# Split products for every expert weight, one two further back: a one-core patch, attention and routed-expert kernel

## Chip, core and metric

The kernel runs on one core of a Trainium2 chip. The metric is the device time in microseconds (us) of one execution; the profile covers one execution, and its span is a little shorter than the time that is reported for it.

## What is computed

The reference, cut to its steps (64 images, 114 tokens each: a class token, 36 patches, 77 text tokens; width 256):

```
h = concat(patches @ W + b with class token + positions, txt)     # 64 x 114 x 256
h = h + linear_attention(layernorm(h))                            # 16 heads, elu + 1
x = layernorm(h); logits = x @ gate_w.T                           # 8 experts
sel = argmax(logits); rw = sigmoid(max(logits))
for e in range(8):                                                # one expert per token
    xs = x * (rw * (sel == e))
    out += (xs @ w_up[e].T) * silu(xs @ w_gate[e].T) @ w_down[e].T
return h + out                                                    # inner width 128
```

## The kernel before

**Stages.** 18 units make the patches. Then a loop of 32 steps (`step(i)` on each engine, all written out) runs the attention of 32 pairs of images as a pipeline: in step i TensorE projects pair i, applies attention to pair i-1, projects pair i-2 out and ranks the experts' choices of pair i-4. The 64 rows of attention output per pair go to a scratch tensor in HBM, sorted by expert, with two indirect DMAs per pair, which GpSimd issues (`scatter`, L674). The last stage walks over 64 tiles of 128 sorted rows, two tiles at a time: a "two" is called `duo` in the code, there are 32 of them (`DUOS`), and `duo_step(j)` is one engine's part of a round. All tiles of one expert lie together, so each tile has one expert, read from a table into registers.

**A two in the last stage.** SyncE loads its two tiles from the scratch. TensorE transposes the rows (`turn_rows`, L1687), ScalarE copies them out rounded (`xsT_hi`, L967), VectorE makes the rest (`xsT_lo`, L995). TensorE multiplies by gate and up (`gate_up`, L1400 to L1402), ScalarE takes the silu of the gate half (L961), VectorE scales the up half and multiplies (`act_of`, L1296). TensorE transposes that (`turn_act`, L1674), ScalarE copies it (`actT`, L956), TensorE multiplies by the down weight (`down`, L1701), VectorE adds the rows (`result_of`, L1308), and GpSimd stores the result with one indirect DMA per tile (L760).

**Split parts.** `product` (L1400 to L1402) writes one float32 product as three products of rounded operands: high by high, high by low, low by high. Before the change it is used everywhere but in `down`, which multiplies in float32; the trace shows two matmul records for each of its products. The high parts of the gate and up weights are made by ScalarE (L874) and the low parts by GpSimd (L683), one of 16 pieces in each of the steps 10 to 25.

**Order.** Nothing schedules: the order on each engine is that of the code, and semaphores hold the engines together. In the last stage TensorE runs in each round gate and up of tile 0, the transposes of the two before, gate and up of tile 1, `down` of the two before, and the transposes of the rows two ahead. The last pairs of the attention and the first twos are interleaved by hand.

**Tables.** When 23 pairs are ranked, a table of the first 32 tiles is made ("early"): VectorE counts in step 27 (`early_count`), and works out row and expert of each tile in steps 28 and 29 (`early_slots`, `early_rows`). SyncE can then load tiles. The other 32 tiles need all pairs: `late_count` on TensorE waits until GpSimd has added up the last choices (`so_far`, L658, in `count_chosen`), then VectorE works out the late table in `late_count`, `late_slots` and `late_rows`. GpSimd's own order at the end of the attention is `scatter` of pair 30, `count_chosen` of pair 31, `scatter` of pair 31, and only then the stores.

## Time and profile before

| | |
|---|---|
| time, median of 3 runs | 437.87 us (436.64 to 438.05) |
| the profiled execution | 436.53 us, span 434.7 us |
| TensorE busy | 412.7 us, 95% of the span |
| VectorE busy | 349.8 us, 80% |
| ScalarE busy | 283.1 us, 65% |
| GpSimd busy | 298.6 us, 69% |
| 64 stores on GpSimd (L760) | 62.3 us busy, 28.4 us idle before them |

How to read it: an engine's busy share is a mean over stages. A row of the timeline gives the start and the length of an operation, and in brackets how long its engine stood idle before it and what ended that. Matmuls overlap, so what a matmul costs TensorE is the distance between starts and not its length.

### The profile page before, as it was taken

What the parts mean: (1) busy time and instruction counts of PE and PEld (TensorE: products, weight loads), DVE (VectorE), ACT (ScalarE), POOL (GpSimd) and SP (SyncE); (2) the same over time, 40 slices, a digit from 0 to 9 for tenths busy, and PEclk for the clock granted to TensorE, in tenths of its full rate; (3) what the DMA queues carried; (4) which work ended last, traced back from release to release, by engine and by line L of the source; (5) the groups of instructions that cost most, each with busy time, mean ns of one, the idle gap of its engine ahead of it and who ended that gap; (6) DMA issues with size and microseconds to landing.
All of it is one profiled execution on the core that took longest, in us unless ns stands there. A gap on an engine that the chain in (4) does not pass through costs nothing.

```text
span 434.7 us, 13221 instructions
## 1 busy us (share of the span) xinstructions
PE 412.7 (95%) x4325; PEld 398.7 (92%) x4325; DVE 349.8 (80%) x1147; ACT 283.1 (65%) x688; POOL 298.6 (69%) x678
## 2 busy tenths in 40 slices
PE   7999999999999999999999999999997999999980
PEld 6999899999999999999999999989896998999970
DVE  5678568999999999999999999998886766766650
ACT  5554476788688788788778778766664554555530
POOL 4065214677878888888888888776677777666662
PEclk9999999999999999999999999999999999999995
DMA  7974122333422321231311211128612797222120
GB/s 268 348 250 146 52 48 57 95 93 94 115 71 67 90 68 40 66 96 39 111 53 36 59 55 40 51 74 226 185 45 69 235 288 238 98 73 72 70 78 14
DMA packets 34148, 46.46 MB, mean 107 GB/s; under 512 B 8842, under 2 KB 25856, under 8 KB 34082
## 3 DMA queue, kind: packets, MB, share of 16 engines
q1 hardware_dynamic: 24860, 30.50, 23.2%
q0 software_dynamic: 9216, 15.12, 11.1%
q8 instruction: 36, 0.59, 0.6%
q14 instruction: 30, 0.25, 0.2%
q10 hardware_dynamic: 6, 0.00, 0.0%
HBM read 26.87 MB, written 17.17 MB: 101 GB/s over the span
## 4 chain that ended last, share of the span: by engine, by line
PE 85%; DVE 5%; issue 4%; ACT 1%; DMA 1%; POOL 1%; POOLq 0%; SPq 0%; DVEq 0%
PE b_kg L1400 8%; PE b_kg L1401 8%; PE b_kg L1402 8%; PE b_w L1400 7%; PE b_w L1401 7%; PE b_w L1402 6%; PE b_att L1515 6%; PE b_t L1465 3%; PE b_w L1701 3%; PE b_v L1402 3%; PE b_v L1400 3%; PE b_v L1401 3%; PE b_att L1701 3%; PE b_att L1452 3%; PE b_t L1529 3%
## 5 line engine op out<-in xcount | busy, mean ns | idle before, releaser
L674 POOL DMA_INDIRECT sorted_rows<-rows,place x64 | 75.5, 1180 | 20.3 <-issue 9.4
L760 POOL DMA_INDIRECT out<-result,rows_all x64 | 62.3, 973 | 28.4 <-DVE result L1308 14.7
L866 ACT ACTIVATE q_exp<-b_w,bq_s 128x228 f32<-128x228 f32 x64 | 28.9, 452 | 28.6 <-PE b_w L1402 28.6
L1400 PE MATMUL b_kg<-wgu_hi,xsT_hi 128*128 x128 | 41.3, 323 | 0.5 <-issue 0.4
L1296 DVE SCALAR_TENSOR_TENSOR act_u<-b_kg,rows_all,silu_g 128x128 f32<-128x128 f32 x64 | 19.4, 345 | 27.1 <-ACT silu_g L961 26.7
L1400 PE MATMUL b_w<-xnT_hi,wq_hi 128*128 128x264 f32 x128 | 39.5, 309 | 1.3 <-DVE logits L1119 1.0
L1400 PE MATMUL b_kg<-wkgv_hi,xnT_hi 128*114 128x264 f32 x128 | 38.7, 302 | 0.4 <-DVE patch_out L1036 0.4
L1401 PE MATMUL b_kg<-wkgv_lo,xnT_hi 128*114 128x264 f32 x128 | 36.5, 285 | 0.0
L1401 PE MATMUL b_w<-xnT_lo,wq_hi 128*128 128x264 f32 x128 | 36.4, 285 | 0.0
L1402 PE MATMUL b_kg<-wkgv_hi,xnT_lo 128*114 128x264 f32 x128 | 36.4, 284 | 0.0
L1402 PE MATMUL b_w<-xnT_hi,wq_lo 128*128 128x264 f32 x128 | 36.4, 284 | 0.0
L1402 PE MATMUL b_v<-wkgv_hi,xnT_lo 128*114 128x256 f32 x128 | 36.0, 282 | 0.0
L1400 PE MATMUL b_v<-wkgv_hi,xnT_hi 128*114 128x256 f32 x128 | 36.0, 281 | 0.0
L1402 PE MATMUL b_kg<-wgu_hi,xsT_lo 128*128 x128 | 35.9, 281 | 0.0
L1401 PE MATMUL b_kg<-wgu_lo,xsT_hi 128*128 x128 | 35.8, 279 | 0.0
L1401 PE MATMUL b_v<-wkgv_lo,xnT_hi 128*114 128x256 f32 x128 | 35.7, 279 | 0.0
L1515 PE MATMUL b_att<-kv_sb,qT 128*114 128x136 f32 x256 | 34.9, 279 | 0.7 <-DVE qT L1097 0.7
L1401 PE MATMUL b_w<-wo_lo,attnT_hi 128*114 128x264 f32 x124 | 35.2, 284 | 0.0
L1400 PE MATMUL b_w<-wo_hi,attnT_hi 128*114 128x264 f32 x124 | 35.2, 284 | 0.0
L1402 PE MATMUL b_w<-wo_hi,attnT_lo 128*114 128x264 f32 x124 | 35.0, 283 | 0.0
L821 ACT ACTIVATE xn<-rows_all,shift,rstd 114x255 f32<-114x255 f32 x64 | 34.7, 596 | 0.0
L1515 PEld LDWEIGHTS b_att<-kv_sb,qT 128*114 128x114 f32 x256 | 31.7, 178 | 1.0 <-DVE kv_sb L1088 1.0
(233 smaller groups left out, 1561.7 us busy)
## 6 DMA issues: line engine op xcount, KB each, us to landing
rows_all<-sorted_rows SPq DMA_DIRECT2D x64, 130.0 KB, 3.2
rows_all<-in_x SPq DMA_DIRECT2D x18, 384.0 KB, 4.7
rows_all<-in_txt SPq DMA_DIRECT2D x32, 154.0 KB
rows_all<-in_wgu_in SPq DMA_DIRECT2D x8, 256.0 KB, 3.0
rows_all<-patch_out SPq DMA_DIRECT2D x48, 36.0 KB
sorted_rows<-tail_rows SPq DMA_DIRECT2D x9, 130.0 KB, 2.9
sorted_rows<-rows,place POOLq DMA_INDIRECT x64, 3.7
wdown<-in_wdown_in SPq DMA_DIRECT2D x2, 512.0 KB, 4.5
```

Source lines behind the costliest of these rows:

```text
L674: G.indirect_dma_start(out=scratch[0:EXPERTS * REGION, :], out_offset=bass.IndirectOffsetOnAxis(ap=place[:, k, b:b + 1], axis=0), in_=rows ...
L760: G.indirect_dma_start(out=out, out_offset=bass.IndirectOffsetOnAxis(ap=rows_all[:, t.n, ID:ID + 1].bitcast(I32), axis=0), in_=result[:, k ...
L821: last = S.activation(xn[:, b, 1:], rows_all[0:TOK, 2 * p + b, 1:D], ACT.Identity, bias=shift1[:, p % 8, b:b + 1], scale=rstd1[:, p % 8, b ...
L866: S.activation(q_exp[:, c, :], at, ACT.Exp, bias=bq_s[:, c:c + 1])
L1296: last = V.scalar_tensor_tensor(act_u[:, t.slot(4)], b_gu[m.slot(2)][:, up:up + INNER], rows_all[:, t.n, GAIN:GAIN + 1], silu_g[:, t.slot( ...
L1400: T.matmul(to, left_hi, right_hi, start=start, stop=False, skip_group_check=seeded)
L1401: T.matmul(to, left_hi, right_lo, start=False, stop=False, skip_group_check=seeded)
L1402: return T.matmul(to, left_lo, right_hi, start=False, stop=stop, skip_group_check=seeded)
L1452: last = T.matmul(b_kv[j * PART:(j + 1) * PART, b * KC + c], k_sb[:, b, at:at + PART], v_sb[:, b, c, j, :], start=True, stop=True)
L1465: last = T.transpose(turn_attn_bank(p)[:, at:at + TOK], attn[:, b, c * P:(c + 1) * P], ident[0:TOK, 0:TOK])
L1515: last = T.matmul(b_att[0:TOK, b, c * KVW:(c + 1) * KVW], qT[:, c, b * TOK:(b + 1) * TOK], kv_sb[:, b * KC + c].rearrange("p j w -> p (j w ...
L1701: last = T.matmul(down_bank(m)[:, t.slot(2) * D:(t.slot(2) + 1) * D], actT[:, t.slot(6)], wdown[:, bass.ds(e, 1), :], start=True, stop=True)
```

## The change

Four things are changed. (1) `down` is also written with `product`: the down weight and the activations get high and low parts. ScalarE copies the high part of one expert's down weight and GpSimd subtracts the low part in each of the steps 21 to 28, and the split of gate and up moves from steps 10 to 25 to steps 5 to 20. The activations' high part is ScalarE's copy after the transpose, and VectorE gets a new operation for the low part (`act_low`). (2) In the last stage `down` and `result_of` run two twos behind gate and up instead of one. Each tile of a two has a bank of its own for gate and up, and GpSimd waits for each tile's result by itself. (3) ScalarE scales both halves (a second activation, Identity), so that VectorE's `act_of` is one multiplication of two operands in SBUF, 128 by 256. (4) The sums of the early table move from VectorE to GpSimd, as additions in halves; `late_count` stands one round later.

```diff
-        wdown = sb("wdown", [P, EXPERTS, D])
-        xsT_lo = sb("xsT_lo", [P, 6, KC, P], F32R)
-        actT = sb("actT", [P, 6, P])
+        wdown_hi, wdown_lo = parts("wdown", [P, EXPERTS, D])
+        up_g = sb("up_g", [P, 4, INNER])
...
+        def gate_up_bank(m, n):
+            return b_kg[:, n, m.slot(2) * 2 * INNER:(m.slot(2) + 1) * 2 * INNER]
...
-        GU_STEPS, DOWN_STEPS = (8, 9, 11, 12, 14, 15, 17, 18), (22, 24)
-        GU_SPLIT_STEPS = range(10, 10 + EXPERTS * KC)
+        GU_STEPS, DOWN_STEPS = (8, 9, 11, 12, 14, 15, 17, 18), (20, 21)
+        GU_SPLIT_STEPS, DOWN_SPLIT_STEPS = range(5, 5 + EXPERTS * KC), range(21, 21 + EXPERTS)
...
 GpSimd
+            def down_low(e):
+                pool.wait_ge(down_hi_done, e + 1)
+                G.tensor_tensor(wdown_lo[:, e, :], down_raw(e), wdown_hi[:, e, :].bitcast(F32), ALU.subtract).then_inc(down_lo_done, 1)
...
+            def early_past():
+                pool.wait_ge(early_past_ready, 1)
+                early_link(G.tensor_tensor(past_n[:], past[:], over_slots(ends[:, 0, EXPERTS:2 * EXPERTS]), ALU.mult), 1)
+            def early_sums():
+                for n, width in enumerate((EXPERTS // 2, EXPERTS // 4, EXPERTS // 8)):
+                    G.tensor_tensor(past[:, :, 0:width], past[:, :, 0:width], past[:, :, width:2 * width], ALU.add)
+                    early_link(G.tensor_tensor(past_n[:, :, 0:width], past_n[:, :, 0:width], past_n[:, :, width:2 * width], ALU.add), 2 + n)
+            def early_rows():
+                early_link(G.tensor_scalar(slot_r[:], past_n[:, :, 0], -float(P), None, ALU.mult), 5)
+                early_link(G.tensor_tensor(slot_r2[:], slot_r[:], slots_s[:, EARLY_TILES * EXPERTS:], ALU.add), 6)
+                early_link(G.tensor_scalar(slot_s[:], past[:, :, 0], float(REGION), None, ALU.mult), 7)
+                early_link(G.tensor_tensor(slot_r[:], slot_s[:], slot_r2[:], ALU.add), 8)
+                G.tensor_copy(slot_row[:, 0:EARLY_TILES], slot_r[:])
+                G.tensor_copy(slot_expert[:, 0:EARLY_TILES], past[:, :, 0]).then_inc(early_ready, 1)
...
+                if i == EARLY_PAIRS + 5:
+                    early_past()
+                if i == EARLY_PAIRS + 6:
+                    early_sums()
+                    early_rows()
...
-                    pool.wait_ge(result_ready, m.upto())
                     for t in tiles_of(m):
                         k = t.slot(RESULT_RING)
+                        pool.wait_ge(result_ready, t.n + 1)
...
 ScalarE
+            def act_high(m):
+                act.wait_ge(turn_a_done, m.upto())
+                if m.had(3):
+                    act.wait_ge(down_done, m.upto(3))
+                S.copy(act_parts(m)[0], turn_a_bank(m)).then_inc(actT_hi_ready, 1)
+            def gate_and_up(m):
+                for t in tiles_of(m):
+                    act.wait_ge(gu_done, t.n + 1)
+                    bank, gain = gate_up_bank(m, t.slot(2)), rows_all[:, t.n, GAIN:GAIN + 1]
+                    S.activation(silu_g[:, t.slot(4)], bank[:, 0:INNER], ACT.Silu, scale=gain)
+                    S.activation(up_g[:, t.slot(4)], bank[:, INNER:], ACT.Identity, scale=gain).then_inc(silu_ready, 1)
             def duo_step(j):
+                if j.within(DUOS):
+                    gate_and_up(j)
                 if (j - 1).within(DUOS):
+                    act_high(j - 1)
                 if (j + 2).within(DUOS):
+                    rows_high(j + 2)
...
 VectorE
-                dve.wait_ge(silu_ready, m.upto())
+                dve.wait_ge(silu_ready, m.upto(per=DUO))
...
-                for t in tiles_of(m):
-                    up = t.slot(2) * D + INNER
-                    last = V.scalar_tensor_tensor(act_u[:, t.slot(4)], b_gu[m.slot(2)][:, up:up + INNER], rows_all[:, t.n, GAIN:GAIN + 1],
-                                                  silu_g[:, t.slot(4)], ALU.mult, ALU.mult)
-                last.then_inc(act_ready, 1)
+                V.tensor_tensor(duo(act_u, m), duo(up_g, m), duo(silu_g, m), ALU.mult).then_inc(act_ready, 1)
+            def act_low(m):
+                dve.wait_ge(actT_hi_ready, m.upto())
+                high, to = act_parts(m)
+                low(to, turn_a_bank(m), high).then_inc(actT_lo_ready, 1)
...
                 if j.within(DUOS):
                     act_of(j)
                 if (j - 1).within(DUOS):
-                    result_of(j - 1)
+                    act_low(j - 1)
+                if (j - 2).had(2) and (j - 2).within(DUOS):
+                    result_of(j - 2)
                 if (j + 2).within(DUOS):
                     rows_low(j + 2)
...
 TensorE
             def gate_up(m, n):
+                if m.had(1):
+                    pe.wait_ge(silu_ready, DUO * (m.n - 1) + n + 1)
...
             def down(m):
-                pe.wait_ge(actT_ready, m.upto())
+                pe.wait_ge(actT_lo_ready, m.upto())
...
-                    last = T.matmul(down_bank(m)[:, t.slot(2) * D:(t.slot(2) + 1) * D], actT[:, t.slot(6)],
-                                    wdown[:, bass.ds(e, 1), :], start=True, stop=True)
+                    last = product(down_bank(m)[:, t.slot(2) * D:(t.slot(2) + 1) * D], [part[:, at] for part in act_parts(m)],
+                                   (wdown_hi[:, bass.ds(e, 1), :], wdown_lo[:, bass.ds(e, 1), :]), True, True)
...
                     first_products(m)
-                    gate_up(m, 0)
+                    for n in range(DUO):
+                        gate_up(m, n).then_inc(gu_done, 1)
                 if (j - 1).within(DUOS):
                     turn_act(j - 1)
-                if m.within(DUOS):
-                    gate_up(m, 1).then_inc(gu_done, 1)
-                if (j - 1).within(DUOS):
-                    down(j - 1)
                 if (j + 2).within(DUOS):
                     turn_rows(j + 2)
+                if (j - 2).had(2) and (j - 2).within(DUOS):
+                    down(j - 2)
...
             down(Turn(0, 1))
             rank(PAIRS - 1)
-            late_count()
             turn_rows(Turn(0, 4))
             duo_step(Turn(0, 3))
+            late_count()
+            duo_step(Turn(0, 4))
             late_slots()
```

How the order moves on TensorE within one round of the last stage. Before, the piece from the end of gate and up to the next transposes of rows (`wdown` is the down weight, `actT` the activations, `con_s` holds the identity with which TensorE transposes, ISA rows compute an address):

```order
L1402 MATMUL b_kg<-wgu_hi,xsT_lo 128x256
L1654 ISA
L1701 MATMUL b_w<-wdown,actT 128x256
L1654 ISA
L1701 MATMUL b_w<-wdown,actT 128x256
L1687 MATMUL b_t<-con_s,rows_all 128x128 x4
L1654 ISA
L1400 MATMUL b_kg<-wgu_hi,xsT_hi 128x256
```

The same place of the changed kernel, from the last product of gate and up to the first of the second tile's down (`wkgv_lo` and `xnT_hi`, `xnT_lo` are the attention's tiles, used again for the rows' low part and for the activations' two parts):

```order
L1493 MATMUL b_kg<-wgu_hi,wkgv_lo 128x256
L1768 MATMUL b_w<-con_s,act_u 128x128 x2
L1781 MATMUL b_t<-con_s,rows_all 128x128 x4
L1745 ISA
L1491 MATMUL b_att<-wdown_hi,xnT_hi 128x256
L1492 REGISTER_ALU
L1492 MATMUL b_att<-wdown_lo,xnT_hi 128x256
L1493 MATMUL b_att<-wdown_hi,xnT_lo 128x256
L1745 ISA
L1491 MATMUL b_att<-wdown_hi,xnT_hi 128x256
L1492 REGISTER_ALU
```

The 12 products of gate and up now stand in one run, both kinds of transposes stand together, and the down products, six where there were two, stand last, of the two before the one whose activations are being transposed.

On TensorE where the attention ends. Before, behind the ranking of the last pair (`chosen`, `so_far`):

```order
L1433 MATMUL b_att<-chosen,earlier 114x16
L1434 MATMUL b_att<-chosen,ones_bf 114x8
L1436 MATMUL b_att<-so_far,ones_bf 114x16 x2
L1734 MATMUL b_att<-so_far,ones_bf 1x8 x2
L1736 MATMUL b_att<-ones_bf,so_far 8x1 x2
L1687 MATMUL b_v<-con_s,rows_all 128x128 x4
```

In the changed kernel, the end of round 3, which stands between that ranking and `late_count`:

```order
L1493 MATMUL b_kg<-wgu_hi,wkgv_hi 128x256
L1768 MATMUL b_w<-con_s,act_u 128x128 x2
L1781 MATMUL b_t<-con_s,rows_all 128x128 x4
L1828 MATMUL b_att<-so_far,ones_bf 1x8 x2
L1830 MATMUL b_att<-ones_bf,so_far 8x1 x2
L1742 TENSOR_LOAD slot_expert
```

The two sums that need the last `so_far` have moved behind the transposes of rows of two 4, the products of two 3, the activations' transposes of two 2 and the rows' transposes of two 5.

On VectorE at the same time. Before, behind the statistics of the last pair (`BN_AGGR`):

```order
L1049 BN_STATS stats<-rows 114x6 x2
L1053 BN_AGGR mv<-stats 114x2 x2
L1296 SCALAR_TENSOR_TENSOR act_u<-b_kg,rows_all,silu_g 128x128 x2
L1308 SCALAR_TENSOR_TENSOR result<-rows_all,b_w 128x256 x2
L995 TENSOR_TENSOR xsT_lo<-b_v,xsT_hi 128x512
```

The same place after the change:

```order
L1141 BN_STATS stats<-rows 114x6 x2
L1145 BN_AGGR mv<-stats 114x2 x2
L1087 TENSOR_TENSOR xnT_lo<-b_w,xnT_hi 128x256
L1375 TENSOR_TENSOR act_u<-up_g,silu_g 128x256
L1391 SCALAR_TENSOR_TENSOR result<-rows_all,b_w 128x256 x2
L1087 TENSOR_TENSOR wkgv_hi<-b_v,xsT_hi 128x512
```

The low part of two 1's activations (`xnT_lo<-b_w`), for which `down` of two 1 waits, stands behind the statistics of the last pair; before, that product waited for ScalarE's copy alone.

## Rows read from the trace of the kernel before

**Rows 1.** Timeline, TensorE, one two: start us, length us, engine, line, operation.

```profile
369.30 0.36 PE L1400 MATMUL b_kg<-wgu_hi,xsT_hi 128*128 x1
369.50 0.28 PE L1401 MATMUL b_kg<-wgu_lo,xsT_hi 128*128 x1
...
370.09 0.38 PE L1674 MATMUL b_w<-con_s,act_u 128*128 128x128 f32 x2
...
371.03 1.12 PE L1701 MATMUL b_w<-wdown,actT 128*128 x4
371.99 0.60 PE L1687 MATMUL b_t<-con_s,rows_all 128*128 128x128 f32 x4
372.35 0.36 PE L1400 MATMUL b_kg<-wgu_hi,xsT_hi 128*128 x1
```

**Rows 2.** Timeline, VectorE, the same two; idle time and its releaser in brackets.

```profile
368.83 0.61 DVE L1296 SCALAR_TENSOR_TENSOR act_u<-b_kg,rows_all,silu_g 128x128 f32<-128x128 f32 x2 [0.98 <-ACT silu_g L961]
369.35 0.86 DVE L1308 SCALAR_TENSOR_TENSOR result<-rows_all,b_att 128x256 f32<-128x256 f32 x2
370.20 0.69 DVE L995 TENSOR_TENSOR xsT_lo<-b_v,xsT_hi 128x512 fp32r<-128x512 f32 x1
```

**Rows 3.** Timeline, ScalarE, the same two.

```profile
370.51 0.37 ACT L956 COPY actT<-b_w 128x256 f32<-128x256 f32 x1 [0.34 <-PE b_w L1674]
371.21 0.63 ACT L961 ACTIVATE silu_g<-b_kg,rows_all 128x128 f32<-128x128 f32 x2 [0.34 <-PE b_kg L1402]
372.63 0.59 ACT L967 CAST xsT_hi<-b_t 128x512 fp32r<-128x512 f32 x1 [0.78 <-PE b_t L1687]
```

**Rows 4.** Timeline, GpSimd: first store, 24th store, last store of 64.

```profile
336.96 1.01 POOL L760 DMA_INDIRECT out<-result,rows_all  x1 [0.30 <-issue]
...
366.40 0.97 POOL L760 DMA_INDIRECT out<-result,rows_all  x1 [0.30 <-issue]
...
426.38 0.97 POOL L760 DMA_INDIRECT out<-result,rows_all  x1 [0.30 <-issue]
```

**Rows 5.** Timeline, TensorE and VectorE, around the wait for so_far.

```profile
327.78 0.25 DVE L1053 BATCH_NORM_AGGREGATE mv<-stats 114x2 f32<-114x6 f32 x2
...
330.62 0.19 PE L1734 MATMUL b_att<-so_far,ones_bf 128*1 128x8 bf16 x2 [2.45 <-POOL so_far L658]
```

**Rows 6.** Chain of waits: the eight products of apply in steps 25, 26 and 30.

```profile
257.20 0.93 PE b_att L1515 x8
...
265.45 0.93 PE b_att L1515 x8
...
300.72 0.93 PE b_att L1515 x8
```

**Rows 7.** Busy time by stretch, VectorE: the early table's parts in steps 28 and 29.

```profile
278.85:280.30 1.45, 1.35 (x9) 1.00 0.00 0
287.95:289.06 1.11, 1.01 (x9) 1.00 0.00 0
```

**Rows 8.** Timeline, GpSimd: a weight's low part, start of step 30, its top_n.

```profile
260.80 0.74 POOL L683 TENSOR_TENSOR wgu_lo<-rows_all,wgu_hi 128x256 fp32r<-128x256 f32 x1
...
296.12 0.23 POOL L635 TENSOR_SCALAR ve<-mv 114x2 f32<-114x2 f32 x1 [0.56 <-DVE mv L1053]
...
301.94 0.20 POOL L650 TENSOR_TENSOR top_n<-top,ratio 114x2 f32<-114x2 f32 x1
```

**Rows 9.** Timeline, ScalarE: a tanh of step 31, the only table load of the late stage.

```profile
305.85 0.24 ACT L805 ACTIVATE tanh_top<-top_n 114x2 f32<-114x2 f32 x1
...
315.50 1.28 ACT L974 ACT_TABLE_LOAD   x1
```

**Rows 10.** Timeline, GpSimd and VectorE: a scatter and a read beside qT.

```profile
280.78 1.25 POOL L674 DMA_INDIRECT sorted_rows<-rows,place  x1 [0.33 <-POOL place L671]
...
280.85 0.62 DVE L1097 SCALAR_TENSOR_TENSOR qT<-q_exp,q_relu 128x456 f32<-128x456 f32 x1
...
306.04 0.64 DVE L1097 SCALAR_TENSOR_TENSOR qT<-q_exp,q_relu 128x456 f32<-128x456 f32 x1
...
306.16 0.58 POOL L642 TENSOR_TENSOR ratio<-spread,rstd 114x2 f32<-114x2 f32 x1
```

More of the change, by code:

```diff
@@ L1382, in _ @@
             stats_2(PAIRS - 1)
-            duo_step(Turn(0, 2))
+            act_low(Turn(0, 1))
+            act_of(Turn(0, 2))
+            result_of(Turn(0, 1))
+            rows_low(Turn(0, 4))
             places(PAIRS - 1)
+            duo_step(Turn(0, 3))
             late_count()
-            duo_step(Turn(0, 3))
+            duo_step(Turn(0, 4))
             late_slots()
-            duo_step(Turn(0, 4))
+            duo_step(Turn(0, 5))
             late_rows()
-            straight(range(5, DUOS + 1), duo_step)
+            straight(range(6, DUOS + 2), duo_step)
         @block.tensor
```

137 lines of the change are left out of this document (79 added, 58 removed).

## The prediction

> **What bounds the kernel now.** I read the timeline of TensorE first, because it is busy for 95% of the span. In the last stage one round (two tiles) lasts from 369.30 to 372.35, which is 3.05 us, without a gap [rows 1]. Inside it, six products of gate and up take 0.79 us (369.30 to 370.09). The next piece, transposes of the activations and six more products, takes 0.94, so the transposes cost 0.15. `down` takes 0.96 (371.03 to 371.99) and the rows' transposes 0.36. The spacing of the products is (370.09 - 369.50) / 5 = 0.118 us, and the first after transposes takes 0.20. VectorE works 0.61 + 0.86 + 0.69 = 2.16 us in such a round and idles 0.98 before one of them [rows 2]. ScalarE works 0.37 + 0.63 + 0.59 = 1.59 us [rows 3].
>
> The second thing to see is GpSimd's stores. The first starts at 336.96, the 24th at 366.40: 29.44 / 23 = 1.280 us each, back to back, although TensorE had produced results before [rows 4]. So GpSimd starts late, behind the last scatters, and catches up, since two stores take 2.56 us and a round 3.05. From then on it follows TensorE. The 64th store starts at 426.38, that is 89.4 us after the first, where 63 x 1.280 = 80.6 would do. The end of the kernel is 434.7 - 426.38 = 8.3 us after that start. Two limits therefore lie close together: 3.05 us per round on TensorE, 2.56 on GpSimd.
>
> The third view is the chain of waits in the loop. From step 25 to 26 the distance of `apply` is 265.45 - 257.20 = 8.25 us; from there to step 30 it is 35.27 instead of 4 x 8.25 = 33.0 [rows 6]. In those steps VectorE makes the early table, in stretches of 1.45 and 1.11 us [rows 7]. VectorE is nearly full in this loop, so the work goes straight into the step. Last, TensorE stands 2.45 us until 330.62 for the last `so_far` [rows 5].
>
> **The change, part by part.**
>
> *Down in split parts, order within a round.* After the change a round on TensorE is 12 products in one run that follows products (12 x 0.118 = 1.42), activations' transposes 0.15, rows' transposes 0.36, and six products behind transposes 0.79: 2.72 us, so 0.33 less than now [rows 1]. Over the 26 rounds from 5 to 31 that is 8.6 us on TensorE alone.
>
> *Will the others keep up with 2.72?* ScalarE gets two more activations. The pair costs 0.63 [rows 3]; two pairs 1.26, with 0.37 and 0.59 that makes 2.22. If the second of each kind did not overlap, four would cost about 1.46 and the sum is 2.42. Silu and Identity alternate per tile; a table load costs 1.28 us, but the only one of this stage is at 315.50 and Identity, Tanh and Silu all follow it without another [rows 9], so I count none. VectorE: `act_of` becomes one operation of 256 columns and `act_low` is one from PSUM of 256. Neither stands in the trace; 512 columns take 0.69 and 128 about 0.31 [rows 2], so each lies between 0.31 and 0.69, and I take 0.41. Sum 0.41 + 0.41 + 0.86 + 0.69 = 2.37 of 2.72. With bounds it is 2.17 to 2.93; only the upper end would be a new limit. The distances between engines get longer by one stage, but `down` now asks for activations of two rounds ago: a chain of silu, `act_of`, transposes, copy and low part (about 0.34 + 1.3 + 0.4 + 0.15 + 0.34 + 0.37 + 0.4 = 3.3 us) has over 5 us. So I keep 2.72 on TensorE.
>
> *The stores.* Now GpSimd needs 2.56 for a round of 2.72, and it starts about three rounds behind. It gains only 0.16 us per round on TensorE, so over 29 rounds it just about catches up. The end is then set by the first store plus 80.6 us, with almost no idle left. I put TensorE's round 5 at about 334.8 and round 31 at 334.8 + 26 x 2.72 + 0.6 (two loads of the tables) = 406.1; the results of two 29 come some 4.1 us later, at 410.2. GpSimd, if it starts at 335.9 (below), wants them at 335.9 + 29 x 2.56 = 410.1. So 0.2 us idle. This replaces 89.4 by 80.8: **-8.6 us**. It also caps the gain: a still faster TensorE would bring nothing.
>
> *Late count moved.* The wait of 2.45 us for `so_far` goes, since two 3 is multiplied in between. What is late next is `act_low` of two 1: it stands on VectorE behind the statistics of the last pair, which end at 327.78 + 0.25 [rows 5]. With 0.41 more, `down` of two 1 starts at 328.45, takes 0.79, and with the ranking TensorE is at the rows of two 4 at 329.4 where it now is at 330.8: -1.4 us. Two 2 is no longer in front of round 4, which shifts work to the end, where TensorE is not the limit. None of this moves the first store, which waits for GpSimd's own scatters; it keeps the results ahead of the stores.
>
> *Early table on GpSimd.* From VectorE go 1.45 + 1.11 us; `early_share` (about 0.6: a small operation and one of 256 elements) comes back. So 2.0 of the 2.27 us lost in steps 26 to 30 can return. But GpSimd pays. A low part costs 0.74 [rows 8], and three more steps get one; the multiplication in step 28 has as many elements per partition, 0.74 too. The halving sums have 128, 64 and 32 elements, twice each; between 0.20 (an operation of two elements) and 0.74 (256) these are about 0.46, 0.33 and 0.26, so 2.1 for the six, four linked small ones at 0.31 and two copies 0.4: with links 3.8 to 4.3 us in step 29. After it GpSimd has only 0.56 us of idle before step 30 [rows 8], so step 30 starts about 3.6 us later than now, and its top_n (301.94) ends at about 305.7. The tanh that needs it runs at 305.85 now [rows 9], and keys and values of step 31 stand behind it on ScalarE. At that point the 1.9 us that VectorE won are held up to the old time; part of it comes back in the idle time that ScalarE has behind it. For the first store I take -1.1 us, with bounds of -2.0 (all is kept) and +1 (GpSimd is later still).
>
> *Costs at nothing.* The down weights' 8 copies on ScalarE and the earlier split of gate and up: hidden by ScalarE's waits for TensorE in each step; if that cover were gone, about 0.4 us per step. The down weights' loads: they leave SyncE's queue behind the text of steps 19 and 20 and are wanted in steps 21 and 25. The later early table lets the first tiles load later; they are wanted after step 31.
>
> **Sum.** First store 336.96 - 1.1 = 335.9; last store + 80.8 = 416.7; + 8.3 = 425.0 us span, which is 9.7 less than 434.7. The profiled execution took 436.53, so 426.8 for its like. The median of the runs lies 1.3 above the profiled one, the lowest run 0.1; I add 0.9 and predict **427.7 us**.
>
> **A lock that speaks against it.** `act_of` now reads both operands from SBUF. What such an operation does to GpSimd shows beside `qT`, which has two SBUF operands as well: GpSimd's `ratio` took 0.58 us beside it (306.16, [rows 10]), where an operation of its form takes 0.20 [rows 8]. A scatter that ran over the whole of another `qT` took 1.25 [rows 10]; I see no stretching of DMA issues. If each store pair were held for the 0.41 us of `act_of`, a round would cost GpSimd 2.97, and the last store would start at 335.9 + 31 x 2.97 + 1.28 = 429.3: 2.9 us later than now.
>
> The Trainium skill, page "SBUF — State Buffer", section "Who interferes with whom", says that a VectorE instruction with two SBUF inputs contends with a GpSimd instruction that reads SBUF, not with one that only writes it, and that whichever came second waits. The stretched `ratio` agrees with it. By its sentence that descriptor generation needs the write side, which it calls inferred, the stores are not held; if their reads of indices counted, the second number holds.
>
> **Rivals.**
> - *As above:* 425.9 to 429.0 us, chance 0.60.
> - *The loop gives nothing or takes.* GpSimd's debt in step 29 holds ScalarE, and the first store stays at 337 or comes at 338: 428.8 to 430. For it: 3.6 us of debt against 0.56 of idle. Against it: the idle times of step 31. Chance 0.17.
> - *The round is longer than 2.72:* at 2.80 to 2.90 the results of two 29 come 2 to 5 us later and GpSimd waits for them: 429.8 to 433. For it: VectorE at its upper bound (2.93). Chance 0.12.
> - *ScalarE becomes the bound and the kernel is slower.* If it does not run ahead and each of its three groups waits the hop from TensorE again (0.34, 0.34, 0.78), the round is 2.42 + 1.46 = 3.9 us. It decides against the change from a round of about 3.35 us on. At 3.5, 27 x 0.45 - 1.4 = 10.8 us are added to TensorE's time: 448. Against it: those waits are there only because ScalarE is ahead. Chance 0.04.
> - *The lock holds the stores:* 437.87 + 2.9 = 440.8 by the number above, chance 0.03.
> - *Nothing comes of it:* six products cost as much as the four records did, and the loop breaks even: 437 to 438.5. Against it: 0.118 per product is measured for the same operands. Chance 0.04.
>
> The measurement of this kernel can tell about 0.3% (1.3 us) from no change. Faster by more: 0.60 + 0.17 + 0.12 and a little of the last, 0.90. Within: 0.03. Slower: 0.07. The range is 425.0 (loop gain kept whole, no starving) to 431.0 (the first of the two slower cases of the gain, half of the next): that leaves out the far half of the third case and those below it.
>
> **What would show it.** In the changed profile: six down products spaced 0.118 apart; rounds of 2.72 on TensorE, with no idle; 64 stores over 80.6 to 81.5 us, each pitch 1.28 with next to no waits for VectorE; the first store at about 335.9; no wait for `so_far` but a wait of some 1.3 us in front of `down` of two 1; `apply` of steps 26 to 30 less than 34 us apart, and ScalarE waiting for top_n in step 31. I am wrong if a pitch above 1.4 stands beside `act_of`, if table loads appear, or if TensorE waits in most rounds for VectorE or ScalarE.

## The result, and the profile after

The changed kernel takes **431.27 us** in the median of 4 executions (430.77 to 431.85), the kernel before 437.44 us beside it; the ratio is 0.986, 95% interval 0.9834 to 0.9885. It is faster, by about 6.2 us. Forecast were 427.7 us, range 425.0 to 431.0. The profiled execution took 431.59 us, its span is 429.8. One execution of the kernel before, of 580.02 us at a granted clock of 0.654, was in a slower state and is left out of every median and ratio.

The page of the changed kernel, its stores group (operation, busy time, mean ns of one, idle time before). Before, the same 64 stores were 62.3 us busy, 973 ns each; now they are 1045 ns each.

```profile
span 429.8 us, 13564 instructions
L831 POOL DMA_INDIRECT out<-result,rows_all x64 | 66.9, 1045 | 19.5 <-issue 12.8
```

The timeline of TensorE for one two of the last stage, in the place of [rows 1].

```profile
381.59 0.28 PE L1491 MATMUL b_kg<-wgu_hi,xsT_hi 128*128 x1
...
383.00 0.38 PE L1768 MATMUL b_w<-con_s,act_u 128*128 128x128 f32 x2
383.22 0.60 PE L1781 MATMUL b_t<-con_s,rows_all 128*128 128x128 f32 x4
383.58 0.37 PE L1491 MATMUL b_att<-wdown_hi,xnT_hi 128*128 x1
...
384.37 0.28 PE L1491 MATMUL b_kg<-wgu_hi,xsT_hi 128*128 x1
```

The round lasts 384.37 - 381.59 = 2.78 us, without a gap: twelve products 1.41, the activations' transposes 0.22, the rows' transposes 0.36, six products of `down` 0.79. The prediction had 1.42, 0.15, 0.36 and 0.79. Every third round takes 2.73, so the mean is 2.76.

VectorE and GpSimd in the same time, in the place of [rows 2, 4].

```profile
381.08 0.42 DVE L1375 TENSOR_TENSOR act_u<-up_g,silu_g 128x256 f32<-128x256 f32 x1 [0.55 <-ACT up_g L1041]
381.42 0.42 DVE L1087 TENSOR_TENSOR xnT_lo<-b_att,xnT_hi 128x256 fp32r<-128x256 f32 x1
381.79 0.87 DVE L1391 SCALAR_TENSOR_TENSOR result<-rows_all,b_w 128x256 f32<-128x256 f32 x2
383.86 0.43 DVE L1375 TENSOR_TENSOR act_u<-up_g,silu_g 128x256 f32<-128x256 f32 x1 [0.60 <-ACT up_g L1041]
```

```profile
381.19 1.16 POOL L831 DMA_INDIRECT out<-result,rows_all  x1 [0.31 <-issue]
382.65 0.97 POOL L831 DMA_INDIRECT out<-result,rows_all  x1 [0.30 <-issue]
383.93 1.20 POOL L831 DMA_INDIRECT out<-result,rows_all  x1 [0.31 <-issue]
```

This is the finding of the case. From 353 to 409 us one store in two is longer; the two shown here by 0.19 and 0.23 us, and they start 0.11 and 0.07 us after an `act_of` (`act_u`, L1375). Two stores now take 2.78 us (383.93 to 381.19 is 2.74, the next pairs 2.78), as long as a round of TensorE.

The first and the last store:

```profile
336.68 1.12 POOL L831 DMA_INDIRECT out<-result,rows_all  x1 [0.30 <-issue]
...
421.80 0.97 POOL L831 DMA_INDIRECT out<-result,rows_all  x1 [0.30 <-issue]
```

So the first store came only 0.28 us earlier than in [rows 4] (forecast 1.1); the 64 took 85.12 us in place of 89.42 (forecast 80.8); behind the last start stand 429.8 - 421.80 = 8.0 us in place of 8.3. Together -4.9 us of span, where -9.7 was forecast. Over all 64 stores, 23 are longer than 1.05 us. Their excess over 0.97 is 4.7 us, about what the 64 take above 63 x 1.28 = 80.6. (What the hold costs is less, since a part of that time would be waits for results without it: experiment 1.)

**The loop.** The product of `apply` in steps 30, 31 and 32, first before, then after.

```profile
300.56 1.09 PE L1515 MATMUL b_att<-kv_sb,qT 128*114 128x136 f32 x8
...
308.78 1.09 PE L1515 MATMUL b_att<-kv_sb,qT 128*114 128x136 f32 x8
...
314.01 1.15 PE L1515 MATMUL b_att<-kv_sb,qT 128*114 128x136 f32 x8 [0.74 <-DVE qT L1097]
```

```profile
299.11 1.09 PE L1606 MATMUL b_att<-kv_sb,qT 128*114 128x136 f32 x8
...
308.36 1.09 PE L1606 MATMUL b_att<-kv_sb,qT 128*114 128x136 f32 x8
...
314.15 1.04 PE L1606 MATMUL b_att<-kv_sb,qT 128*114 128x136 f32 x7 [1.30 <-DVE qT L1189]
```

(In the last row one of the eight records is missing.) Up to step 30 the loop has won 1.45 us; two steps later nothing is left. GpSimd and ScalarE between the two show why:

```profile
295.60 0.45 POOL L737 TENSOR_TENSOR past<-past 1x128 f32<-1x128 f32 x1
...
299.62 0.22 POOL L747 CAST slot_expert<-past 1x32 int32<-1x32 f32 x1
...
300.25 0.23 POOL L667 TENSOR_SCALAR mean_neg<-mv 114x2 f32<-114x2 f32 x1
```

```profile
300.51 0.91 ACT L882 ACTIVATE rows<-rows,mean_neg 114x256 f32<-114x256 f32 x2 [1.85 <-POOL mean_neg L667]
```

The sums and rows of the early table take GpSimd from 295.60 to 299.84, 4.24 us. The small operation `mean_neg` of the next step stands behind them, and ScalarE stands 1.85 us for it.

**Where the attention ends.** TensorE and VectorE at the place of [rows 5], then the busy times by stretches of 2 us (the last three columns are the granted clock, the DMA share and GB/s).

```profile
328.34 0.38 PE L1491 MATMUL b_w<-wdown_hi,xnT_hi 128*128 x1 [2.05 <-DVE xnT_lo L1087]
```

```profile
327.63 0.25 DVE L1145 BATCH_NORM_AGGREGATE mv<-stats 114x2 f32<-114x6 f32 x2
327.79 0.39 DVE L1087 TENSOR_TENSOR xnT_lo<-b_w,xnT_hi 128x256 fp32r<-128x256 f32 x1
```

```profile
328.00:330.00 2.00, 1.66 (x15) 1.67 (x16) 1.16 (x4) 0.00 (x0) 1.70 (x2) 0.93 0.15 36
330.00:332.00 2.00, 2.00 (x11) 2.00 (x10) 1.09 (x6) 1.49 (x3) 1.74 (x7) 0.50 0.28 76
```

The wait for `so_far` is gone. In its place TensorE waits 2.05 us for the low part of two 1's activations, which stands behind the last statistics, as foretold (forecast 1.3). Behind that wait the granted clock is 0.50 for two microseconds, the level of 1.2 GHz, and the products of round 3 stand 0.21 us apart instead of 0.118. That round takes 3.97 us (329.74 to 333.71), where it takes 2.42 in experiment 1, whose clock stays at 1.00 here.

### The profile page after: what moved, and what is told of

The parts are those of the page before. It is cut to its first block, busy times and chain, and to the rows that moved or that the text cites. A ratio compares the mean times of both kernels' runs of the same rounds, so it can differ in the third digit from the quotient of the medians.

```text
span 429.8 us, 13564 instructions
## 1 busy us (share of the span) xinstructions
PE 406.6 (95%) x4389; PEld 399.4 (93%) x4389; DVE 352.1 (82%) x1140; ACT 298.8 (70%) x760; POOL 312.0 (73%) x699
## 4 chain that ended last, share of the span: by engine, by line
PE 83%; POOL 5%; issue 4%; DVE 3%; ACT 2%; DMA 1%; POOLq 0%; SPq 0%; DVEq 0%; ACTq 0%
PE b_kg L1491 8%; PE b_kg L1492 8%; PE b_kg L1493 8%; PE b_w L1491 8%; PE b_w L1492 7%; PE b_w L1493 7%; PE b_att L1606 6%; PE b_t L1556 3%; PE b_v L1493 3%; PE b_v L1491 3%; PE b_v L1492 3%; PE b_t L1620 3%; PE b_att L1543 3%; PE b_att L1491 3%; PE b_att L1493 2%
## 5 line engine op out<-in xcount | busy, mean ns | idle before, releaser
L831 POOL DMA_INDIRECT out<-result,rows_all x64 | 66.9, 1045 | 19.5 <-issue 12.8
L1040 ACT ACTIVATE silu_g<-b_kg,rows_all 128x128 f32<-128x128 f32 x64 | 23.5, 368 | 21.8 <-PE b_kg L1493 19.6
L1491 PE MATMUL b_kg<-wgu_hi,xsT_hi 128*128 x128 | 37.2, 290 | 0.0
L882 ACT ACTIVATE rows<-rows,mean_neg 114x256 f32<-114x256 f32 x64 | 29.2, 509 | 2.2 <-POOL mean_neg L667 2.2
```

The source lines that it names most:

```text
L831: G.indirect_dma_start(out=out, out_offset=bass.IndirectOffsetOnAxis(ap=rows_all[:, t.n, ID:ID + 1].bitcast(I32), axis=0), in_=result[:, k ...
L882: last = S.activation(rows[:, p % 4, b, 0:D], rows[:, p % 4, b, 0:D], ACT.Identity, bias=mean_neg[:, p % 4, b:b + 1])
L1040: S.activation(silu_g[:, t.slot(4)], bank[:, 0:INNER], ACT.Silu, scale=gain)
L1491: T.matmul(to, left_hi, right_hi, start=start, stop=False, skip_group_check=seeded)
```

## The experiments

The first theory was that the 256-column `act_of`, with both operands in SBUF, holds a store that starts beside it, and that GpSimd then falls into step with the round. Its rival was that something else lengthens the stores. A second question was the loop. All medians are of 4 executions unless it says otherwise; the kernel before ran beside them at 437.34, 437.73 and 437.48 us. The medians of one kernel's four executions spread over 0.5 to 2.5 us, so differences of a few tenths between medians say nothing.

**1. Part 3 undone.**

```diff
-                    S.activation(up_g[:, t.slot(4)], bank[:, INNER:], ACT.Identity, scale=gain)
...
-                V.tensor_tensor(duo(act_u, m), duo(up_g, m), duo(silu_g, m), ALU.mult)
+                for t in tiles_of(m):
+                    last = V.scalar_tensor_tensor(act_u[:, t.slot(4)], gate_up_bank(m, t.slot(2))[:, INNER:], rows_all[:, t.n, GAIN:GAIN + 1],
+                                                  silu_g[:, t.slot(4)], ALU.mult, ALU.mult)
```

One bank again holds gate and up of both tiles of a two, and ScalarE waits for the products of both. So this edit changes more than the operands of `act_of`; experiment 5 changes the operation alone.

> The changed kernel with part 3 undone: VectorE scales the up half from PSUM again (two operations of 128 columns, one SBUF and one PSUM operand each), ScalarE only takes the silu, and gate and up of a two share a bank. Theory 1 (the two-SBUF-operand multiplication holds every other store, and so chains GpSimd's 2.56 us of stores to TensorE's round of 2.78): no store beyond 1.05 us, pitch 1.28 throughout, 64 stores in about 80.7 us instead of 85.1, span about 4.3 us shorter than 429.8, time 427 us. Theory 2 (the stores are stretched by something else that came with the change, the DMA traffic or the wait for each tile): 1.20 us stores stay, time 431 us. Theory 3 (TensorE's round of 2.78 alone sets the end): stores get short but wait for results, time 431 us.

Measured: 429.74 us (428.97 to 430.56), ratio 0.983 (0.9803 to 0.9857). VectorE and GpSimd of this kernel:

```profile
380.46 0.61 DVE L1375 SCALAR_TENSOR_TENSOR act_u<-b_kg,rows_all,silu_g 128x128 f32<-128x128 f32 x2 [0.42 <-ACT silu_g L1040]
```

```profile
381.42 0.98 POOL L831 DMA_INDIRECT out<-result,rows_all  x1 [0.30 <-issue]
382.70 0.97 POOL L831 DMA_INDIRECT out<-result,rows_all  x1 [0.30 <-issue]
383.98 0.98 POOL L831 DMA_INDIRECT out<-result,rows_all  x1 [0.30 <-issue]
385.36 0.97 POOL L831 DMA_INDIRECT out<-result,rows_all  x1 [0.41 <-DVE result L1393]
```

No store of the 64 is longer than 1.05 us. They take 82.61 us from first to last, 2.5 less. GpSimd catches up with the results and from there waits for them, 2.0 us in all (the last row above has 0.11 of it). The round is 2.79. So the hold costs 1.5 us in the medians and 2.5 in the stores of the two profiles, and what remains above 80.6 is TensorE: the results come too late for stores back to back. Theory 2 is out. Theories 1 and 3 each have a part: the time lies between their 427 and 431.

**2. Part 3 alone, on the kernel before.** The same edit in the other direction, `up_g` in the memory of a tile that the attention has done with.

> The kernel before with part 3 alone: ScalarE scales both halves and VectorE multiplies two SBUF operands of 256 columns. Theory 1: stores of up to 1.4 us appear (held for up to the 0.42 us of the multiplication); GpSimd catches up more slowly or not at all on rounds of 3.05 us, so the last store comes 0 to 5 us later than before: 437.5 to 443 us. Theory 2: no stretched store, time as before, 437.4 us.

Measured: 438.43 us (437.51 to 439.28, 10 executions) against 437.34 (13), ratio 1.0023 (1.0006 to 1.004). VectorE and GpSimd:

```profile
382.10 0.43 DVE L1296 TENSOR_TENSOR act_u<-kv_sb,silu_g 128x256 f32<-128x256 f32 x1 [1.22 <-ACT kv_sb L964]
```

```profile
381.07 0.97 POOL L761 DMA_INDIRECT out<-result,rows_all  x1 [0.73 <-DVE result L1306]
382.35 1.03 POOL L761 DMA_INDIRECT out<-result,rows_all  x1 [0.30 <-issue]
```

Here the second store starts 0.25 us after `act_of` and is longer by only 0.06. Two more were caught at 0.10 and 0.19 us and took 1.17 and 1.08. With the stores of the changed kernel this gives one law: a store that starts d us after such an `act_of` is longer by about 0.30 - d (0.07: 1.20; 0.11: 1.16; 0.25: 1.03), and one that starts before it or later is not. While GpSimd catches up, a round of 3.05 against two stores of 2.56 lets the store drift by 0.49 us per round, so it steps over the stretch of 0.30; with a round of 2.78 the drift is 0.22, it is caught, and the hold just makes up the difference. That is why GpSimd stays in step and never catches up.

Once GpSimd has caught up in this kernel, 16 more stores sit at 0.22 to 0.25 us after an `act_of` and are longer by 0.05 to 0.08. That costs nothing, because GpSimd waits for results there (8.6 us in all, 9.0 in the kernel before). The 1.1 us between the medians are therefore not shown to be the hold's: in its profile TensorE stands 2.27 us for `so_far`, the clock falls to 0.54 behind that, and its last round begins 0.6 us later than in the kernel before (418.31 and 417.69).

**3. The early sums and rows on GpSimd one step later.**

```diff
-                if i == EARLY_PAIRS + 6:
+                if i == EARLY_PAIRS + 7:
                     early_sums()
                     early_rows()
```

> The changed kernel with GpSimd's sums and rows of the early table one step later (step 30, in which it has no normalisation of a further pair to make). Theory A (GpSimd's 4.3 us in step 29 hold ScalarE's centring in step 30 for 1.85 us, and give the loop's gain back): that wait vanishes, apply of step 31 comes at about 307.3 instead of 308.4 and the first store 0.7 to 1.5 us earlier, time about 430.3 us. Theory B (the first store is set by the chain of top_n, tanh and scatter after the loop, whatever the loop gained): the wait vanishes, but the first store stays at 336.7, time 431.3 us.

Measured: 430.55 us (430.18 to 431.49), ratio 0.9848 (0.9822 to 0.9873). GpSimd, TensorE:

```profile
296.18 0.22 POOL L667 TENSOR_SCALAR mean_neg<-mv 114x2 f32<-114x2 f32 x1
...
335.51 1.15 POOL L831 DMA_INDIRECT out<-result,rows_all  x1 [0.30 <-issue]
```

```profile
307.49 1.09 PE L1606 MATMUL b_att<-kv_sb,qT 128*114 128x136 f32 x8
...
312.97 1.15 PE L1606 MATMUL b_att<-kv_sb,qT 128*114 128x136 f32 x8 [1.00 <-DVE qT L1189]
```

Theory A holds. `mean_neg` comes 4.1 us earlier, `apply` of step 32 at 312.97 instead of 314.15, and the first store 1.17 us earlier. The loop's gain is real and was given back by the place of GpSimd's sums. The stores still take 85.08 us, 23 of them held.

**4. `down` as one float32 product again, of the high parts alone**, the rest of the change kept. It leaves out the low parts of the down weights and activations.

> The changed kernel with down as one float32 product of the high parts alone (the low parts are made but not multiplied, so that the output is that of rounded operands). TensorE's round gets longer, by 0.96 - 0.79 = 0.17 or a little more, to 2.95 to 3.0. Theory 1 (a store cannot pass the multiplication of two SBUF operands, so GpSimd falls into step with the round): the pair of stores stretches with it to 2.95, by about 0.4 on one of the two. Theory 2 (a fixed surcharge from other traffic): pairs stay at 2.78, and GpSimd catches up with TensorE and waits for results.

Measured: 433.38 us (one execution). A round is 2.93 us. The stores take 86.97:

```profile
379.67 0.97 POOL L831 DMA_INDIRECT out<-result,rows_all  x1 [0.69 <-DVE result L1391]
380.95 0.97 POOL L831 DMA_INDIRECT out<-result,rows_all  x1 [0.30 <-issue]
```

Only 3 of 64 are held, since the drift is 2.93 - 2.56 = 0.37, more than 0.30. GpSimd passes through and then waits 5.9 us for results. Neither expectation holds as put: the stores don't stretch to the round, and no fixed surcharge stays either. What fits is a hold of at most 0.30. The three products instead of float32 are worth 2.93 - 2.78 = 0.15 us a round.

**5. `act_of` as two operations of 128 columns**, operands still in SBUF.

```diff
-                V.tensor_tensor(duo(act_u, m), duo(up_g, m), duo(silu_g, m), ALU.mult)
+                for t in tiles_of(m):
+                    last = V.tensor_tensor(act_u[:, t.slot(4)], up_g[:, t.slot(4)], silu_g[:, t.slot(4)], ALU.mult)
```

> The changed kernel with VectorE's multiplication of two SBUF operands as two operations of 128 columns instead of one of 256. In the changed kernel a store that begins p us after the multiplication is longer by 0.27 - p, so that at most 0.27 us are added, more than the 0.22 us by which a round (2.78) exceeds two stores (2.56). Theory 1 (the store waits for the multiplication under way): the most that can be added is about 0.13 us, less than 0.22, so the stores no longer fall into step with the round; fewer than 10 stretched stores, the last store at 418.5 to 420 instead of 421.8, time 429 to 430 us. Rival (any such operation in that place stretches every other store): 23 stretched stores again, 431.3 us.

Measured: 429.72 us (428.80 to 430.63), ratio 0.9816 (0.9777 to 0.9855). VectorE, and GpSimd beside it:

```profile
381.01 0.50 DVE L1376 TENSOR_TENSOR act_u<-up_g,silu_g 128x128 f32<-128x128 f32 x2 [0.53 <-ACT up_g L1041]
```

```profile
380.78 0.97 POOL L831 DMA_INDIRECT out<-result,rows_all  x1 [0.30 <-issue]
382.06 0.97 POOL L831 DMA_INDIRECT out<-result,rows_all  x1 [0.31 <-issue]
```

The one held store starts 0.26 us after an `act_of`, so 0.06 us into its second half:

```profile
372.98 1.08 POOL L831 DMA_INDIRECT out<-result,rows_all  x1 [0.30 <-issue]
```

One store is longer than 1.05 us, 82.63 us from first to last, 1.8 us of waits for results: the same as with `act_of` from PSUM. This kernel keeps the same operands and work and only shortens the longest hold. The stores that start inside its 0.5 us show it: at 0.15 and 0.19 us they take 0.99 and 0.97, at 0.26, 0.32 and 0.44 us 1.08, 1.02 and 0.98. So each half releases a store about 0.17 us after its own start, and 0.17 is less than the drift of 0.22. The theory holds. It also shows that a store that runs already when `act_of` starts (380.78, `act_of` at 381.01) is not lengthened.

**6. The low part of two 1's activations ahead of the last statistics** (`act_low(Turn(0, 1))` and `stats_2(PAIRS - 1)` change places on VectorE).

> The changed kernel with the low part of two 1's activations ahead of the statistics of the last pair on VectorE. Theory (TensorE's wait of 2.05 us in front of down of two 1 is for that order, and the granted clock of 0.50 between 330 and 332 follows from the wait): the wait falls to about 1.0 us, products of round 3 are 0.118 us apart again, round 5 begins about 1.5 to 2.5 us earlier. For the end: if the stores are in step with the round, the whole line moves up by a part of that, time 429.5 to 431 us; if only the number of stores mattered, 431.3 us. Rival on the clock: it falls without that wait too.

Measured: 431.36 us (430.88 to 431.63), ratio 0.9849 (0.9815 to 0.9883): nothing against the changed kernel. `down` of two 1 waits 1.18 instead of 2.05 us, and the stand is found one round on. ScalarE, TensorE:

```profile
331.15 0.91 ACT L882 ACTIVATE rows<-rows,mean_neg 114x256 f32<-114x256 f32 x2 [1.39 <-POOL mean_neg L667]
332.58 0.20 ACT L876 ACTIVATE tanh_top<-top_n 114x2 f32<-114x2 f32 x1 [0.52 <-POOL top_n L681]
```

```profile
333.44 0.38 PE L1491 MATMUL b_kg<-wgu_hi,xsT_hi 128*128 x1 [2.05 <-ACT up_g L1041]
```

The scaling of two 3, which frees the bank for the products of two 4, stands on ScalarE behind the last pair's attention work. That work waits for GpSimd, whose `mean_neg` stands behind its scatters, and comes at the same time as in the changed kernel (331.15; 331.07 there). So whatever TensorE wins before, it waits for the same moment. The granted clock stays at 1.00 behind both stands, the one of 1.18 and the one of 2.05 us. So of the expectation only the shorter wait and the 0.118 us came true; round 5 begins 0.3 us earlier (336.60 for 336.87), not 1.5 to 2.5.

**7. The early table back on VectorE (part 4 undone for it).**

> The changed kernel with the early table on VectorE as before (part 4 undone). Theory A (GpSimd pays back what VectorE wins in the loop): apply of step 30 comes at 300.6 instead of 299.1, but step 31 and the transition at the same time as in the changed kernel or earlier, the first store at 336.2 to 337, time 431 to 432 us. Rival (the early table on GpSimd was a gain or a loss of its own): a difference of over 1 us either way.

Measured: 431.35 us (431.22 to 432.54), ratio 0.985 (0.9818 to 0.9883). Theory A holds: as it stands, moving the early table is worth nothing. Its profiled execution was later by about 1 us from the first steps of the loop on, so the times within it aren't set against the others.

**8. Three edits together** (1, 3 and 6).

> The three edits together: VectorE reads the up half from PSUM (act_psum), GpSimd's sums one step later (sums_step30), the low part of two 1 first (low1_first). First store at about 335.4, no stretched store, TensorE about 2 us further ahead in round 5, so that the stores wait hardly: last store 335.4 + 81.0 = 416.4, span 424.5, time about 426.5 us. If the gains do not add (the last store follows TensorE's rounds of 2.78 in any case): 428.5 us.

Measured: 427.92 us (427.56 to 429.25), ratio 0.977 (0.9737 to 0.9803). Its profiled execution is the slowest of the four, 1.4 us later from the first steps of the loop on. No store is held, 82.64 us from first to last. That is 1.4 us above what was expected and 0.6 below the rival's 428.5. GpSimd still waits 2.2 us for results.

**9. The same without edit 6.**

> act_of from PSUM as before the change, and the early sums one step later, with the low part of two 1's activations left behind the last statistics. Theory (the order of that low part costs nothing in the end, because TensorE's lead is lost one round later anyway): the same median as with all three edits, 427.6 to 428.4. Rival (where the stores are not held, results are what GpSimd waits for, so a stand of 2 us of TensorE before down of two 1 and a fallen clock behind it show in the end): 428.7 to 429.5.

Measured: 428.26 us (427.92 to 428.68), ratio 0.9787 (0.9745 to 0.9829). The place of that low part is worth nothing that can be told here either (0.3 us); the first theory holds. Against experiment 1 the later sums give 1.5 us.

**10. Halves instead of PSUM** (3, 5 and 6).

> The changed kernel with three edits: act_of as two operations of 128 columns, the early table's sums and rows on GpSimd one step later, and the low part of two 1's activations ahead of the last pair's statistics. Theory (the 256-column act_of holds the stores; the sums in step 29 hold the last attention steps): first store 335.5 to 335.9, 64 stores over 82.6 us, a span near 426.1 and a median of 427.5 to 428.3, the same as with act_of from PSUM (427.92). Rival (what helps is that act_of does not read two operands from SBUF at all, and not its length): stores stretched again, 85 us, median near 430.3.

Measured: 428.60 us (427.70 to 430.24), ratio 0.979 (0.9745 to 0.9836). Two stores are held by 0.22 us together, so the rival is out; the median is 0.3 above the range of the theory. The stores of the profiled execution take 84.02 us and not 82.6: its granted clock is 0.60 from 334 to 338, and GpSimd waits 3.3 us for results instead of 1.8. The four executions fall in two pairs: 427.70 and 427.85 us with a mean granted clock of 0.989, 430.24 (the profiled one) and 429.36 with 0.985.

**11. `late_count` back ahead of round 3**, with edit 1.

> act_of from PSUM as before the change, and late_count back where it stood, ahead of round 3 and of the transposes of rows of two 4. Theory (the wait for the last so_far returns and with it some 1.4 us on TensorE, and GpSimd, which already waits 2.0 us for results with act_of from PSUM, waits 1 to 1.5 us longer): 430.7 to 431.3 against 429.74. Rival (two 3 was in time anyway, since TensorE stands for so_far in the time in which it would stand for VectorE's low part): 429.3 to 430.2.

Measured: 430.42 us (429.91 to 431.41), ratio 0.9846 (0.9803 to 0.989). TensorE:

```profile
329.22 0.38 PE L1493 MATMUL b_w<-wdown_hi,xnT_hi 128*128 x1 [2.10 <-DVE xnT_lo L1086]
...
331.35 0.19 PE L1828 MATMUL b_att<-so_far,ones_bf 128*1 128x8 bf16 x2 [0.88 <-POOL so_far L689]
```

It falls between the two expectations. Both waits now stand, 2.98 us, since the first covers most of the second. But GpSimd waits for results as long as in experiment 1 (1.9 and 2.0 us), and the stores take 82.44 us. The loop of this execution was 0.9 us later from its first steps on. With edit 1, then, moving `late_count` back costs 0.7 us between medians whose executions overlap, and the profile shows no loss of it in the stores.

**12. The early table back on VectorE, with edit 1**, where the stores are not held.

> act_of from PSUM, and the early table back on VectorE as before the change. In the changed kernel moving the early table back gave no difference (431.35 against 431.27). Theory (what VectorE gains by step 30 is given back in step 31, and the first store is the same): 429.3 to 430.2, against 429.74. Rival (a difference was there and was swallowed by the held stores): 430.5 to 431.5.

Measured: 429.55 us (429.31 to 429.80), ratio 0.9819 (0.9777 to 0.9861), against 429.74. So experiment 7 did not lose a difference in the held stores: there is none to be seen.

## Why the prediction was wrong in its size

**The failed step: "I see no stretching of DMA issues", and the term of -8.6 us for the stores that rests on it.** The lock stood in the prediction, priced at 0.41 us per round and given a chance of 0.03. It is there, and its price is another: at most 0.30, and in this kernel what two stores lack to a round, 0.22 us. Thus it could never bring the 440.8 us, but it keeps the pitch of two stores at the round. The error was to ask for the whole length of `act_of` or nothing. Experiments 1 and 5 show the cause by two roads, experiment 2 on the other kernel.

**What [rows 10] could have told.** Its scatter could not decide whether stores are held: it began 0.07 us before `qT`, and such a store is not held. Its 1.25 us is no stretching either, since the first scatter of a pair takes 1.24 or 1.25 us nearly everywhere. But the size of a hold stands in its `ratio`, which began 0.12 us after `qT` and took 0.58 instead of 0.20 us. It was released 0.50 us after the start of `qT` and not at its end, 0.64. Of the nine `qT` of the kernel before from 245 us on, eight released a small operation of GpSimd 0.48 to 0.51 us after their start (the ninth stands beside that scatter), for instance:

```profile
254.29 0.62 DVE L1097 SCALAR_TENSOR_TENSOR qT<-q_exp,q_relu 128x456 f32<-128x456 f32 x1
```

```profile
254.30 0.66 POOL L640 COPY rows<-mv 114x2 f32<-114x2 f32 x1
```

The copy takes 0.19 us elsewhere, so it was released 0.48 us after the start of `qT`. The release comes 0.12 to 0.14 us before the recorded end, in `qT` as in `act_of` (0.42 long, 0.30) and in its half (0.29 long, 0.17). Taken off the 0.41 us of the prediction, that gives a hold of 0.29. It is more than the 0.16 us which two stores lacked to the forecast round of 2.72, so the lock-step could have been forecast from rows of before, had stores been taken to be held at all.

The Trainium skill, page "SBUF — State Buffer", section "Who interferes with whom", says that whichever comes second waits, and marks as inferred that `tensor_tensor` takes only the read interface of the shared pair, while descriptor generation needs the write interface. The first half agrees with these runs: the store that begins inside `act_of` waits until about 0.30 us after its start, the one that runs already does not. The inferred half does not agree: with both operands in SBUF `act_of` holds the stores, and with one of them in PSUM (experiment 1) it writes the same tile and holds none. What the store needs in that time is not shown.

**TensorE's results came later: the second part of the same term.** With the hold taken away, GpSimd waits 2.0 us for results in experiment 1, where 0.2 was reckoned. So had the hold not been there, the stores would have taken 82.6 and not 80.8 us. Of the 4.3 us by which the term of -8.6 was too large, the hold is 2.5 and this is 1.8. Round 31 begins at 408.16 in experiment 1, where 406.1 was forecast. Of these 2.1 us, 0.8 are there when round 5 begins (335.62 for 334.8), and 1.2 come in the 26 rounds from 5 to 31, which take 72.5 us for 71.3. That is the third rival's mechanism in small. A part of it is the activations' transposes, 0.22 and not 0.15 us. They now stand in front of the rows' transposes instead of between products; that this is why is not shown.

In the changed kernel itself the -1.4 us for `late_count` were there at the rows of two 4, which begin at 329.34 (forecast 329.4). But round 3 then took 3.97 us, at a clock of 0.50, and round 5 begins at 336.87 and not at 334.8. That is still 1.5 us earlier than in the kernel before (338.38). As the stores are held, this does not decide the end there.

**The first store: -1.1 forecast, -0.28 measured.** This is the second rival, and its mechanism was named: the debt in step 29 was 4.24 us (forecast 3.8 to 4.3), and GpSimd began step 30 with 299.93, 3.8 us later than in [rows 8] (forecast 3.6). Wrong was the place: ScalarE did not stand for top_n in step 31 but for `mean_neg`, near the beginning of step 30, and that took back all of the 1.45 us and not a part. Experiment 3 shows it: -1.17 us for the first store.

**What held.** Six `down` products 0.118 us apart; no idle time of TensorE in the rounds; no further table load; `apply` of steps 26 and 30 33.8 us apart (265.31 and 299.11); the wait for `so_far` gone and a wait before `down` of two 1 in its place, which was 2.05 and not 1.3 us, because the gate and up products in front of it were done at 326.3, where 328.45 - 1.3 = 327.15 had been reckoned. That this wait costs nothing at the end fits experiments 6 and 9, where it is shortened or not to the same median within 0.3 us.

**The sum.** Against the forecast span of 425.0 the stores are +4.3, the first store +0.8, the tail -0.3: 429.8. The 0.9 us that were added for the median did not come; here the median is 0.3 below the profiled execution; that this makes the miss smaller is luck. The measured 431.27 lies 0.27 above the range. Without the hold it would have been inside (429.74), but still 2.0 above the forecast. The range had been cut where half of the third rival was still inside, but neither two rivals together nor a hold smaller than the priced one had a place in it. (The 448 us of the rival on ScalarE should read 448.7, from 437.87 + 10.8.)

**A version that beats both:** `act_of` from PSUM or in halves, and the early sums one step later. The lowest median is that of experiment 8 with 427.92 us, 3.4 below the changed kernel; the order of the low part can be left as it is (428.26).

## What to carry to other kernels

When two engines with nearly the same period share something, reckon with the drift between them and not with the mean: a hold as large as the drift locks them together, and the slack that was to pay for catching up is gone. Here 0.30 against a drift of 0.22 us locked, 0.30 against 0.37 and 0.49 did not, and neither did 0.17 against 0.22. Halving the operation that holds was enough. Work that is moved to an engine with spare time should stand behind the small operations of the next step for which others wait, and not ahead of them.

## What the runs showed of the hardware

GpSimd's indirect stores are held by a VectorE multiplication with two SBUF operands of 256 columns, if they start within about 0.30 us of its start, until about that point: by 0.23 us at 0.07, 0.19 at 0.11, 0.06 at 0.25. With two operations of 128 columns that point is about 0.17 us after the start of each, and beside `qT` with 456 columns GpSimd's small operations are released after 0.48 to 0.51 us: each time 0.11 to 0.14 us before the end that the profile records. A store that starts 0.01 to 0.05 us before the multiplication is not held. A small operation can be: `rows<-route_w,rstd` at 289.49 in the kernel before, 0.12 us ahead of a `qT`, took 0.79 instead of 0.19 us. The multiplication itself shows no loss beside a store (0.42 to 0.43 us either way).

At the end of the attention 13 of the 14 profiles have a stand of TensorE of 1.94 to 2.45 us. In seven of them the granted clock fell behind it, to between 0.50 and 0.56 over a stretch of 2 us (the changed kernel, 2.05 us; experiments 2, 3, 4, 7, 10 and 12, 2.27, 2.08, 1.94, 2.06, 2.07 and 2.04) and stayed at 1.00 in six (the kernel before, 2.45; experiments 1, 5, 6, 9 and 11, 2.11, 2.04, 2.05, 2.07 and 2.10). The stretches of experiments 1 and 12 side by side:

```profile
330.00:332.00 2.00, 2.00 (x22) 1.80 (x20) 0.93 (x6) 1.36 (x3) 1.74 (x7) 1.00 0.27 72
```

```profile
330.00:332.00 2.00, 2.00 (x11) 2.00 (x10) 1.00 (x3) 1.15 (x3) 1.74 (x7) 0.50 0.32 87
```

In the same 2 us TensorE starts 22 matmuls in the one and 11 in the other. What decides between them stays open; the length of the stand alone does not. It does not show in the medians of these two (429.74 and 429.55), though only one execution of each has a profile. In experiment 10, where GpSimd waits for results and the fall comes as late as 334 to 338, the two executions with the lower mean clock are the slower ones, by 1.5 to 2.5 us. Open too is why the loop of some profiled executions begins 1 us and more later than that of others with the same code up to there (first `apply` at 58.67 us in experiment 1, at 60.16 in experiment 8).
